# Graph convolution with residual norm: a quad's loads and stores cut into ten pieces paced by TensorE, square root and norm three runs later

## The reference

```python
edge_index = jnp.stack([src, dst])            # 200000 edges, sorted by dst
row, col = edge_index[0], edge_index[1]       # x is 12500 x 128, float32
h_self = x @ W_lin + b_lin
messages = x[col] @ W_msg + b_msg
msg_sum = jax.ops.segment_sum(messages, row, num_segments=n_nodes)
counts = jax.ops.segment_sum(jnp.ones((row.shape[0],)), row, num_segments=n_nodes)
h_agg = msg_sum / jnp.maximum(counts, 1.0)[:, None]
h = relu(jnp.concatenate([h_self, h_agg], axis=1) @ W_upd + b_upd)
y = x + h
out = (y - mean(y)) / sqrt(var(y) + 1e-5)     # over the last axis
```

## Time and profile before

| | us |
|---|---|
| median of 3 runs | 1282.43 |
| lowest, highest | 1266.48, 1290.02 |
| the profiled execution | 1267.35 |
| its span, first to last instruction | 1265.6 |
| PE busy (matmuls) | 1083.6 |
| DVE busy | 942.5 |
| ACT busy | 769.3 |
| POOL busy | 522.7 |

### The profile page before, as it was taken

How to read it: one execution, slowest core, us unless ns; L and a number is a source line. 1 busy time by engine, 2 the same in 40 slices (tenths; PEclk the granted TensorE clock), 3 DMA queues, 4 the chain that set the end, 5 groups by cost and what they waited for, 6 DMA issues and landing times. The chain is left out here.

```text
span 1265.6 us, 51991 instructions
## 1 busy us (share of the span) xinstructions
PE 1083.6 (86%) x21321; PEld 965.2 (76%) x21321; DVE 942.5 (74%) x2190; ACT 769.3 (61%) x1827; POOL 522.7 (41%) x502
## 2 busy tenths in 40 slices
PE   1939889888697499998988889998999899999996
PEld 0939889887687387887778777877877778888785
DVE  7999999999999756666665666665665556666674
ACT  0313333331111398888877777887887778888885
POOL 3000000000000477666665655665665556666660
PEclk9969989989898699999999998999999999999998
DMA  8212322311340434444444433443444344444430
GB/s 112 80 54 90 117 94 101 106 66 31 111 121 3 118 86 115 105 105 101 104 101 100 103 84 76 101 100 83 104 101 98 95 100 104 104 104 103 104 77 14
DMA packets 121290, 116.27 MB, mean 92 GB/s; under 512 B 35291, under 2 KB 103896, under 8 KB 120983
## 3 DMA queue, kind: packets, MB, share of 16 engines
q1 hardware_dynamic: 95548, 64.96, 19.4%
q0 software_dynamic: 23024, 47.31, 16.4%
q10 hardware_dynamic: 2490, 0.67, 0.3%
HBM read 89.79 MB, written 23.10 MB: 89 GB/s over the span
## 5 line engine op out<-in xcount | busy, mean ns | idle before, releaser
L1286 PE MATMUL slot<-big 32*128 32x384 bf16 x7925 | 744.7, 327 | 53.6 <-issue 29.5
L567 ACT ACTIVATE big<-slot 128x384 bf16<-128x384 f32 x1600 | 666.6, 496 | 147.3 <-PE slot L1286 126.4
L1299 PE MATMUL acc<-big 32*128 32x385 bf16 x6400 | 710.4, 328 | 10.6 <-issue 8.9
L1286 PEld LDWEIGHTS slot<-big 32*128 32x128 bf16 x7925 | 475.7, 93 | 107.7 <-ACT big L567 32.9
L633 POOL DMA_INDIRECT big<-x,dst_at x400 | 425.8, 1064 | 268.2 <-PE acc L1312 176.9
L1299 PEld LDWEIGHTS acc<-big 32*128 32x128 bf16 x6400 | 438.6, 94 | 46.5 <-issue 25.2
L1312 PE MATMUL acc<-big 32*128 32x385 bf16 x1600 | 358.0, 328 | 0.0
L955 DVE TENSOR_TENSOR big<-col_lo,iota_lo 128x512 bf16<-128x512 f16 x400 | 149.9, 416 | 238.9 <-PE acc L1299 237.0
L1324 PE MATMUL acc<-big 32*128 32x385 bf16 x600 | 196.3, 327 | 5.1 <-issue 5.1
L627 POOL MEMSET big<- 128x8 bf16 x4 | 0.2, 100 | 410.3 <-issue 410.3
L943 DVE TENSOR_SCALAR big<-big,iota_k 128x2048 bf16<-128x2048 f16 (+8 forms) x225 | 155.1, 718 | 1.2 <-issue 1.2
(11 more groups left out here) (150 smaller groups left out, 830.7 us busy)
## 6 DMA issues: line engine op xcount, KB each, us to landing
big<-rows SPq DMA_DIRECT2D x100, 128.0 KB
big<-in_x SPq DMA_DIRECT2D x48, 256.0 KB, 3.0
x<-big SPq DMA_DIRECT2D x24, 384.0 KB, 2.6
big<-x,dst_at POOLq DMA_INDIRECT x400
base<-big SPq DMA_DIRECT2D x24, 256.0 KB, 2.5
big<-base SPq DMA_DIRECT2D x24, 256.0 KB
out<-big SPq DMA_DIRECT2D x24, 256.0 KB
big<-x SPq DMA_DIRECT2D x8, 168.0 KB, 2.9
```

The source lines that it names most:

```text
L567: act.activation(xg[R % NX][:, i, 0:F3], slot[i // 2][:, i % 2, 0:F3], ACT.Copy).then_inc(s["xg_ready"], 1)
L1286: ins = nc.tensor.matmul(slot[lane // 2][:, lane % 2, 0:F3], W[q % NW_][rows, hot_at(g, k), :], xwin[rows, WIN_AT[g] + k, :], start=k == 0 ...
L1299: ins = nc.tensor.matmul(acc[lane][:, 0:F3 + 1], l_of(R, i)[rows, :], xg[R % NX][rows, i, 0:F3 + 1], start=r == 0 and i == 0, stop=last an ...
```

## The change

Two numbers move the root and the norm of the quad before: ACT takes the square root after run 11 instead of run 8, DVE scales and shifts at run 12 instead of run 9. The layer stays at run 7.

SP's loop is written anew. Each load of `x4` and `base4` and each store is cut into halves of 256 nodes (128 KB), and the four pieces of index rows are issued one by one. Ahead of each piece SP waits until PE has added up a set number of runs of the current quad (`at_run`): `x4` at 2 and 3, `base4` at 5 and 6, the index rows of quad q + 2 at 8, 9, 10 and 11, the store of quad q - 1 at 13 and 15. `x4` and `base4` of quad q are now loaded in quad q itself; before, they were loaded in quad q - 1. The counts that DVE waits for are doubled, since two halves land.

```diff
@@ -271,7 +271,7 @@
 
 
         ORDER = [g for a in range(RUNS // 2) for g in (a + RUNS // 2, a)]
-        LAYER, ROOT, NORM = 7, 8, 9
+        LAYER, ROOT, NORM = 7, 11, 12
 
         def l_of(R, i):
 
@@ -370,17 +370,14 @@
             for c in range(CP):
                 load_window(c)
 
-            def load_brow(q):
-                if q >= NB:
-                    sp.wait_ge(s["W_ready"], q - NB + 1)
-                for lane in range(4):
-                    rows = rows_dram[q * 4:q * 4 + 4, lane, :, :].rearrange("h g n -> h (g n)").unsqueeze(0).to_broadcast([SL, 4, RUNS * SL])
-                    sp.dma_start(brow[q % NB][lane * SL:(lane + 1) * SL, :, :, :].rearrange("p g h n -> p h (g n)"), rows).then_inc(brow_loaded[q % NB], 16)
-
+            def load_brow(q, lane):
+                rows = rows_dram[q * 4:q * 4 + 4, lane, :, :].rearrange("h g n -> h (g n)").unsqueeze(0).to_broadcast([SL, 4, RUNS * SL])
+                sp.dma_start(brow[q % NB][lane * SL:(lane + 1) * SL, :, :, :].rearrange("p g h n -> p h (g n)"), rows).then_inc(brow_loaded[q % NB], 16)
 
             sp.wait_ge(s["T_made"], U)
             sp.wait_ge(s["rows_stored"], 16 * NROWS)
-            load_brow(0)
+            for lane in range(4):
+                load_brow(0, lane)
 
             sp.wait_ge(s["flag_known"], 1)
             flag = sp.value_load(flag_i[0:1, 0:1], min_val=0, max_val=1)
@@ -388,36 +385,59 @@
             def fast():
                 sp.wait_ge(s["lo_taken"], LISTS_TO[NSL])
 
-                def load_x4(q):
+                def halves(q, half, of):
+
+                    if q < Q - 1:
+                        at = (q * 4 + 2 * half) * P
+                        return slice(0, P), slice(2 * half, 2 * half + 2), of[at:at + 2 * P, :].rearrange("(h p) f -> p h f", p=P)
+                    n = (N - q * 4 * P) // P
+                    at = (q * 4 + half * n) * P
+                    end = at + n * P if half == 0 else N
+                    if half == 0:
+                        return slice(0, P), slice(0, n), of[at:end, :].rearrange("(h p) f -> p h f", p=P)
+                    return slice(0, end - at), slice(n, n + 1), of[at:end, :].unsqueeze(1)
+
+                def load_half(to, of, done, q, half):
                     if q >= 2:
                         sp.wait_ge(s["normed"], q - 1)
-                    n = min(N - q * 4 * P, 4 * P) // P
-                    for to, of, done in ((x4, x, x4_loaded), (base4, base_dram, base4_loaded)):
-                        sp.dma_start(to[q % 2][:, 0:n, :], of[q * 4 * P:(q * 4 + n) * P, :].rearrange("(h p) f -> p h f", p=P)).then_inc(done[q % 2], 16)
-                        if q == Q - 1:
-                            rest = N - (q * 4 + n) * P
-                            sp.dma_start(to[q % 2][0:rest, n, :], of[(q * 4 + n) * P:N, :]).then_inc(done[q % 2], 16)
-
-                def store(q):
+                    rows, hs, there = halves(q, half, of)
+                    sp.dma_start(to[q % 2][rows, hs, :], there).then_inc(done[q % 2], 16)
+
+                def store_half(q, half):
                     sp.wait_ge(s["normed"], q + 1)
-                    n = min(N - q * 4 * P, 4 * P) // P
-                    sp.dma_start(out[q * 4 * P:(q * 4 + n) * P, :].rearrange("(h p) f -> p h f", p=P), O[q % 2][:, 0:n, :]).then_inc(stored[q % 2], 16)
-                    if q == Q - 1:
-                        rest = N - (q * 4 + n) * P
-                        sp.dma_start(out[(q * 4 + n) * P:N, :], O[q % 2][0:rest, n, :]).then_inc(stored[q % 2], 16)
+                    rows, hs, there = halves(q, half, out)
+                    sp.dma_start(there, O[q % 2][rows, hs, :]).then_inc(stored[q % 2], 16)
+
+                def at_run(q, r):
+
+                    sp.wait_ge(s["aggregated"], q * RUNS + r)
 
                 sp.wait_ge(s["W_ready"], 1)
-                load_brow(1)
-                load_x4(0)
-                load_x4(1)
+                load_brow(1, 0)
+                load_brow(1, 1)
+                at_run(0, 1)
+                load_brow(1, 2)
+                load_brow(1, 3)
                 for q in range(Q):
-                    if q + 2 < Q:
-                        load_brow(q + 2)
-                    store(q)
-                    if q + 2 < Q:
-                        load_x4(q + 2)
-                sp.wait_ge(stored[0], 16 * ((Q + 1) // 2 + 1))
-                sp.wait_ge(stored[1], 16 * (Q // 2))
+                    for half, r in ((0, 2), (1, 3)):
+                        at_run(q, r)
+                        load_half(x4, x, x4_loaded, q, half)
+                    for half, r in ((0, 5), (1, 6)):
+                        at_run(q, r)
+                        load_half(base4, base_dram, base4_loaded, q, half)
+                    for lane in range(4):
+                        if q + 2 < Q:
+                            at_run(q, 8 + lane)
+                            sp.wait_ge(s["W_ready"], q + 1)
+                            load_brow(q + 2, lane)
+                    for half, r in ((0, 13), (1, 15)):
+                        if q > 0:
+                            at_run(q, r)
+                            store_half(q - 1, half)
+                store_half(Q - 1, 0)
+                store_half(Q - 1, 1)
+                sp.wait_ge(stored[0], 32 * ((Q + 1) // 2))
+                sp.wait_ge(stored[1], 32 * (Q // 2))
 
             def general():
                 sp.wait_ge(s["f_pads"], 4)
@@ -988,7 +1008,7 @@
 
                 def add_constant(q):
                     dve.wait_ge(s["sums_taken"], 2 * q + 2)
-                    dve.wait_ge(base4_loaded[q % 2], 16 * (q // 2 + (2 if q == Q - 1 else 1)))
+                    dve.wait_ge(base4_loaded[q % 2], 32 * (q // 2 + 1))
                     k = mark(nc.vector.tensor_tensor(base4[q % 2], base4[q % 2], const_rep.unsqueeze(1).to_broadcast([P, 4, F]), ALU.add))
                     after(k)
                     for h in range(4):
@@ -1002,7 +1022,7 @@
                         dve.wait_ge(s["normed"], q)
                     dve.wait_ge(s["constant_added"], q + 1)
                     dve.wait_ge(s["counts_turned"], q + 1)
-                    dve.wait_ge(x4_loaded[q % 2], 16 * (q // 2 + (2 if q == Q - 1 else 1)))
+                    dve.wait_ge(x4_loaded[q % 2], 32 * (q // 2 + 1))
                     for h in range(4):
                         ins = nc.vector.scalar_tensor_tensor(out=Y[:, h, :], in0=S[:, h, :], scalar=cnt[:, 1, h:h + 1], in1=base4[q % 2][:, h, :], op0=ALU.mult, op1=ALU.add)
                     ins.then_inc(s["S_read"], 1)
@@ -1022,7 +1042,7 @@
                     after(k)
                     k = mark(nc.vector.scalar_tensor_tensor(out=shift[:, :], in0=mv[:, :, 0], scalar=-1.0, in1=rstd[:, :], op0=ALU.mult, op1=ALU.mult))
                     if q >= 2:
-                        dve.wait_ge(stored[q % 2], 16 * (q // 2))
+                        dve.wait_ge(stored[q % 2], 32 * (q // 2))
                     after(k)
                     for h in range(4):
                         ins = nc.vector.tensor_scalar(O[q % 2][:, h, :], Y[:, h, :], rstd[:, h:h + 1], shift[:, h:h + 1], ALU.mult, ALU.add)
```

## The result

The changed kernel takes 1186.56 us (median of four runs, 1186.32 to 1187.18); the kernel before took 1282.37 in the same comparison. The ratio is 0.935, with a 95% interval of 0.930 to 0.940. I had forecast 1188 within 1176 to 1220. The spread shrank too: before, single runs lay between 1266 and 1290; these four agree within 1 us, and four more of the same kernel (run 10) lie between 1184.2 and 1189.1.

A forecast was written before the change was run, and what follows sets the result against it. PE, the busiest engine, was taken to lose time to instruction blocks held behind SP's bursts and to the root's wait: 1267.35 - 16 - 69 + 5 + 1.6 (first quad) = 1189, by quads 1187.8, taken as 1188 us, range 1176 to 1220.

The forecast's parts named there:

- The sum by quads: Whole kernel: 431.5 + 31.0 + 23 x 29.6 + 42.7 (last quad and tail) + 1.75 = 1187.8 us.
- The root: ACT's square root moved three runs later in the quad loses its wait: 0.7 us per quad, 16 us gained.
- The bursts: SP's once-per-quad loads and stores: spreading them gains 2.88 x 24 = 69 us, of which 5 us stay.
- That PE starves for instruction blocks: Quad stage: PE's 43.5 us of "issue" idle means it ran out of instructions; inferred, not labelled by the profile.
- That a block stands behind whatever is queued: DMA queues: PE's next instruction block waits behind SP's whole 1.28 MB burst, once per quad.
- rival 2: Bursts are not the cause of PE's stalls; only the root's wait goes: 1251 us, chance 0.07.
- The added waits: SP's waits for PE's count ahead of each piece: cost 0; bound 2 us per quad if one is late.
- The norm behind the root: DVE's later norm waits under a run for the root: cost taken as 0, without cover 1.9 us per quad.
- The median: The changed kernel's median should lie at its profiled time, not 15 us above as before.
- Half of the stalls staying: Gathers and pieces together still hold blocks up, 1.4 instead of 0.2 us per quad: 1217 us, chance 0.18.
- the slower case: Each instruction fetch can meet a piece, so every block is late: 1340 us, chance 0.03.
- The root's move giving nothing: The pieces work but moving the root gains nothing: 1188 + 16 = 1204 us, chance 0.05.

The follow-up runs named there:

- run 10: The changed kernel measured again, nothing altered, as a measure for the others: 1186.8 us (1184.2 to 1189.1).
- run 2: The changed kernel with layer, root and norm put back to runs 7, 8, 9 of a quad, so the pieces alone: 1212.0 us.
- run 3: The changed kernel with all ten 128 KB pieces of a quad waiting for run 13, so they go out in one burst: 1184.7 us.
- run 5: The kernel before without POOL's gathers from the second quad on, burst left as it was: 1211.2 us (2 runs).
- run 9: The kernel of run 1 with every 256 KB load and store cut into two of 128 KB, burst start unchanged: 1195.6 us.
- run 1: The kernel before with only root and norm moved to 11 and 12, SP's burst of whole transfers kept: 1229.5 us.
- run 11: The kernel of run 1 with one more wait: the store and the burst behind it begin at PE's run 13: 1194.5 us.
- run 6: The changed kernel with a 128 KB DRAM-to-DRAM copy added behind each of the ten pieces of every quad: 1202.6 us (2 runs).
- run 8: The kernel of run 3 with x, base and store as whole 256 KB transfers, same order, burst at run 13: 1193.4 us.
- run 12: The kernel of run 8 with the store moved to the head of its burst of whole transfers: 1198.4 us.
- run 13: Not an experiment: one of the 16 runs in each quad of the kernel, whose adding up by PE a burst can wait for; no time of its own.

## Why the prediction was right, and where it was not

The time came out 1.4 us from the forecast, but by luck in part: two errors of the sum offset each other, and one step of the mechanism was too simple. The sum by quads, measured, is 434.0 + 31.8 + 676.7 + 43.0 + 1.7 = 1187.2. The quads were 4 us shorter than forecast, and the start of the stage (434.0 for 431.5) and the first quad (31.8 for 31.0) gave 3 back; the start lies between 431.5 and 434.5 in the profiles of all runs here, so it is no effect of the change.

*The root* (0.7 per quad, 16 us): the mechanism was right and the size too small. ACT's wait and the short PE waits are gone, and run 2 prices them at 0.96 per quad, 22 us (25 by the medians). The term was mis-sized because I took the last quad, 29.4, as the quad with nothing in its way. Quads of the changed kernel take 29.1 when nothing holds them. PE's listed waits on ACT in run 2, 15.1 us, are 0.66 per quad; the other 0.3 of the cost stands in no wait row.

*The bursts* (69 less 5 that stay, 64 us): 58 us by run 2 (62 by the medians), and with the overlap of the two parts no single figure is theirs alone: after the root has moved, the pieces bring 43 more (1229.5 to 1186.6). Idle time and clock went together as forecast, from 43.5 us of "issue" to 1.3, and no half clock is left between the first quad and the tail. Quads came out at 29.42 where I had put 29.6: a residue of 0.3 over the shortest ones of 29.1, on a lower floor than I had assumed.

*That PE starves for instruction blocks* was inferred. It is now well borne out: 18 of 19 stops end 2.5 to 3.2 us behind the start of a block, and where blocks come in time PE doesn't stop. No run takes the blocks away, so it is not shown by an edit of its own.

*That a block stands behind whatever is queued* is the step that failed. Run 3 puts the whole 1.28 MB in one burst and has no stalls, and run 5 keeps the burst of before and loses the gathers, and has hardly any. Three edits each take most of the stalls away: halves (run 9 against run 1), a start tied to PE's run and 2.4 us later (run 11 against run 1), no gathers (run 5 against the kernel before). So the long stalls need whole transfers of 256 KB, gathers beside them, and a start at a certain place in the quad, each shown in one of the two kernels: halves and the later start were tried only with the root already moved, the missing gathers only with it at its old place. The forecast survives this, since the change cuts into halves and starts its pieces elsewhere as well as spreading them.

The Trainium skill's rule that a DMA engine takes queues in turn, packet by packet ("DMA: Bandwidth & Descriptors", section on queues, rings and completion order), on which I had based rival 2, fits the runs better than my own picture did: with halves a burst of full length lets the blocks pass, and the trace of run 3 agrees with it, at 6.1 us for the longest interval about a burst. It doesn't account for up to 10.9 us between blocks with whole transfers. The rule that instruction fetch is hidden ("Runtime: NRT & Kernel Launch", section on instruction fetch mechanics) doesn't hold here, if the reading of the stops is right: 43.5 us of PE's idle time before.

*The added waits* cost nothing, as forecast: run 3 and the changed kernel, with quite different waits, differ by 2 us. *The norm behind the root*: DVE waited 2.9 us in two waits for the standard deviation over the whole run, and PE for no node test. *The median* fell to the profiled time, as I had thought. That the 15 us between them before were stalls is inferred; no execution at that length was profiled.

*The rivals.* Half of the stalls staying (1217) and the slower case (1340) are out by the time itself, and run 6 shows how much room there was: it doubles the pieces' bytes and costs 16 us. That the bursts are not the cause (1251) is out by run 2, where the pieces alone bring 58 to 62 us. The root's move giving nothing (1204) is out by run 2 as well.

What stays open is why the start matters. In the nine microseconds from SP's first issue of the burst on POOL issues 7.0 gathers on the mean in the kernel before and 6.6 in run 1, against 5.0 in run 11, 4.8 in run 8 and 4.5 in run 12. A burst at run 13 has fewer gathers beside it, which with run 5 is a likely reason and no proof: counted from a microsecond earlier the figures are 6.2, 6.9 and 5.6 for the kernel before, run 1 and run 11. In run 1 the start also wanders more from quad to quad (24.1 to 31.6 us after the first eviction, against 27.8 to 31.7). The share of the clock's dips in the 58 us wasn't tried alone either.

## What to carry to other kernels

An engine's idle time with no releaser deserves a look at the instruction queue: hold its blocks against the restarts, and if they keep a fixed distance, the engine most likely starves for instructions. Where data transfers crowd the same stretch, cut large transfers and move their start, before building a finer schedule. Here one line that ties a burst to PE's run and one that moves the root give 1194.5 us, halves in such a burst 1184.2 and 1184.7, and ten paced waits, 1186.6 and 1186.8, are no better than that.

Take as the price of a clean stretch the shortest ones of several, not the one that happens to look empty. And a result that meets the forecast can still stand on a wrong step: only the run that undid the pacing alone showed it.

## What the hardware showed that I had not expected

- PE, with 238 recorded instructions per block of 16 KB, had a block every 5.2 us in the changed kernel, and before it restarted 2.5 to 3.2 us after a late block began, though the block's own packet takes about 1.1 us in the trace.
- The same 1.28 MB beside the same gathers, with x, base and store in transfers of 256 or of 128 KB, gave 1229.5 and 1195.6 us.
- In the kernel before, the DMA engines were over 80% busy for 4.5 to 7 us on end at every burst (counted in steps of half a microsecond, median 5.5), and most bursts had a stop of PE behind them. In run 8 the median is 6.0 and no "issue" wait is longer than 1.1 us; in run 3 it is 4.5 (2 to 7.5). The busy share alone doesn't tell a burst that stops PE from one that doesn't.
